# Roots refined on GpSimd, head scales applied to k, normalisation on ScalarE and a three-part output projection in a windowed-attention kernel

## The reference

```
_gn(v):    32 groups of 8 channels; (g - mean) / sqrt(var + 1e-5) per image and group
xw     = roll(x, -4, -4), cut into 8 x 8 windows: 4 windows per image, N = 64 tokens each
q, k   = xw @ Wq.T, xw @ Wk.T          (16 heads of 16 channels);   v = xw @ Wv.T + bv
qn, kn = q / max(|q|, 1e-12), k / max(|k|, 1e-12)
logits = (qn . kn) * exp(min(logit_scale, log 100)) + 16 * sigmoid(bias(head, n, m))
logits = -inf where the shifted-window mask says so;  scores = softmax(logits)
z      = (scores @ v) @ Wo.T + bo, rolled back
```

## Time and profile before

| | |
|---|---|
| median of 3 runs | 882.07 us (876.42 to 893.16) |
| the profiled execution: its own time | 888.09 us |
| its span, first to last instruction | 885.6 us |
| mean granted TensorE clock | 0.956 |
| busy share of the span: PE, PEld | 87%, 74% |
| busy share: DVE, ACT, POOL | 68%, 51%, 52% |

### The profile page before, as it was taken

The page is one execution under the profiler, slowest core; times in us unless marked ns, Lnnn a source line. Parts: engine busy times, 40 slices in busy tenths (PEclk is TensorE's granted clock), DMA queues, the critical chain, the costliest instruction groups (busy, mean ns, idle before and its releaser), DMA issues.

```text
span 885.6 us, 38114 instructions
## 1 busy us (share of the span) xinstructions
PE 767.5 (87%) x15258; PEld 654.2 (74%) x15258; DVE 606.6 (68%) x1641; ACT 453.1 (51%) x848; POOL 457.3 (52%) x584
## 2 busy tenths in 40 slices
PE   3086899999999999997999999999999999999985
PEld 2065778777877787776788887787778777788874
DVE  5164677777767777776777777777777777777641
ACT  2143555555555555653555555555655555555540
POOL 2015546555655665555466555565556555665540
PEclk9576999999999999998999999999999999999995
DMA  5706520000000000000000000000000000000000
GB/s 113 137 12 95 163 61 0 0 0 0 0 0 0 0 0 0 0 3 2 3 3 4 15 26 15 24 24 24 24 12 24 24 24 12 24 26 27 26 28 28
DMA packets 17197, 22.13 MB, mean 25 GB/s; under 512 B 7097, under 2 KB 8418, under 8 KB 17122
## 3 DMA queue, kind: packets, MB, share of 16 engines
q1 hardware_dynamic: 16578, 20.31, 8.8%
q10 hardware_dynamic: 544, 0.79, 0.3%
HBM read 12.68 MB, written 8.42 MB: 24 GB/s over the span
## 4 chain that ended last, share of the span: by engine, by line
PE 62%; DVE 15%; issue 9%; ACT 9%; SPq 3%; DMA 1%; ACTq 1%; DVEq 0%
PE ps_qk L365 21%; PE ps_mix L477 15%; PE ps_qk L489 12%; PE ps_score L450 9%; DVE ps_score L709 5%; ACT squares L553 4%; ACT seed L597 3%; PE ps_mix L467 2%; PE ps_score L410 2%; DVE ps_score L725 2%; DVE ps_score L727 2%; DVE ps_score L729 2%; ACT q_own L575 1%; DVE exp_bias L688 1%; DVE g_off L746 1%
## 5 line engine op out<-in xcount | busy, mean ns | idle before, releaser
L913 POOL TENSOR_TENSOR probs<-probs,exp_bias 128x512 f32<-128x512 f32 x256 | 326.4, 1306 | 267.5 <-ACT probs L612 257.5
L612 ACT ACTIVATE probs<-ps_score,lower 128x512 f32<-128x512 f32 x256 | 155.1, 689 | 128.2 <-PE ps_score L450 128.2
L365 PE MATMUL ps_qk<-w_qk,xn 128*128 128x512 f32 x768 | 205.0, 418 | 0.6 <-POOL xn L892 0.6
L365 PEld LDWEIGHTS ps_qk<-w_qk,xn 128*128 128x128 f32 x768 | 147.3, 199 | 32.3 <-POOL xn L892 0.7
L477 PE MATMUL ps_mix<-v_ones,probs 64*64 64x17 f32 x8064 | 134.3, 209 | 6.5 <-issue 6.5
L477 PEld LDWEIGHTS ps_mix<-v_ones,probs 64*64 64x64 f32 x8064 | 127.6, 136 | 8.7 <-issue 6.7
L553 ACT ACTIVATE squares<-ps_qk 128x512 f32<-128x512 f32 x128 | 76.6, 599 | 109.3 <-PE ps_qk L365 109.3
L398 PE MATMUL ps_mix<-mixed,w_o 128*128 128x256 f32 x512 | 131.0, 400 | 1.4 <-ACT mixed L567 1.4
L450 PE MATMUL ps_score<-q_own,k_rows 32*64 32x128 f32 x4096 | 78.4, 281 | 57.9 <-DVE g_off L746 56.8
L489 PE MATMUL ps_qk<-w_v,xn 128*128 128x256 f32 x768 | 109.4, 293 | 20.3 <-DVE unit L761 20.3
L450 PEld LDWEIGHTS ps_score<-q_own,k_rows 32*64 32x64 f32 x4096 | 63.4, 132 | 82.5 <-DVE g_off L746 50.1
(11 more groups left out here) (74 smaller groups left out, 766.7 us busy)
## 6 DMA issues: line engine op xcount, KB each, us to landing
x_all<-in_x SPq DMA_DIRECT2D x32, 256.0 KB, 2.9
out<-x_out SPq DMA_DIRECT2D x32, 256.0 KB, 2.0
bias_rev<-table_scratch SPq DMA_DIRECT2D x32, 56.5 KB
probs<-in_L_matrices ACTq DMA_DIRECT2D x1, 512.0 KB, 3.7
x_out<-in_L_matrices SPq DMA_DIRECT2D x1, 512.0 KB, 12.0
w_o<-in_L_matrices SPq DMA_DIRECT2D x4, 128.0 KB
probs<-in_L_matrices ACTq DMA_DIRECT2D x1, 256.0 KB, 4.2
allowed<-in_L_matrices SPq DMA_DIRECT2D x1, 256.0 KB, 11.7
```

Source lines behind the costliest of these rows:

```text
L365: last = nc.tensor.matmul(ps_qk[:, e, :], xn[:, px, t.parity, c, e * P:(e + 1) * P], w_qk[:, pw, t.layer, c, :], start=(c == 0 and i == 0) ...
L612: nc.scalar.activation(probs[:, t.parity, r, :, :, :, :].rearrange("p e c a n -> p (e c a n)"), ps_score[:, r, :], ACT.Exp, bias=lower[:, ...
L913: nc.gpsimd.tensor_tensor(pr, pr, exp_bias[:, t.layer, r, :, :, :, :].rearrange("p e c a n -> p (e c a n)"), ALU.mult).then_inc(weighted, 1)
```

## The change

Six edits come together.

1. `newton` moves to GpSimd, between `split_xn` and `weigh`. It has four tensor_tensor operations on up to 66 columns in place of three, on SBUF tiles (`sums_sq`, `seed`, `refined`, `root`, `threes`), each waiting for the one before, and one more for the group offset `g_off`. The squares are taken of twice the value, so that root = (3 - 4 s y^2) y needs no halves. `score` no longer waits for the roots.
2. The head scales are no longer folded into the roots (`scale_norms` is gone); `keep_k` multiplies the transposed k by them, one number per partition. `make_unit` does the clamp and the product in one operation.
3. `normalise` moves from VectorE to ScalarE, after the four `exp`.
4. `project_out` takes three rounded parts: 8 float32r products with the high part of `mixed`, then 4 with its low part, which a new VectorE operation `keep_rest` makes. The output weights are rounded on ScalarE and split on VectorE.
5. Orders: ScalarE does both `keep_q` ahead of `log_sums` and `seed_roots`; VectorE does both residuals ahead of `make_unit`. TensorE's `project_v` stands ahead of `mix` as it did.
6. Loops hold four iterations per pass (4 to 23 and 38 to 57). x2 and x3 are loaded ahead of the bias gathers, x4 too; the tables of both layers begin in the prelude, and `find_table(1)` of ScalarE, the rounding and the splits of layer 1 move to iteration 3.

The core of the diff:

```diff
@@ run
-                first = (4, IMAGES + 6)[layer]
-                last = IMAGES * (layer + 1) - 6
-                with engine.Fori((first + JOBS * exact) // 2, (last + JOBS * exact) // 2) as half:
-                    for parity in range(2):
-                        iteration(first + parity, Job(half, parity, None, exact))
-                some(last, last + (12, 10)[layer])
+                first, last, after = ((4, 24, IMAGES + 6), (IMAGES + 6, 58, JOBS + 4))[layer]
+                with engine.Fori((first + JOBS * exact) // 4, (last + JOBS * exact) // 4) as quarter:
+                    for k in range(4):
+                        half, parity = divmod(first % 4 + k, 2)
+                        iteration(first + k, Job(2 * quarter + half, parity, None, exact))
+                some(last, after)
@@ sync
-            load_table(0)
+            for l in range(LAYERS):
+                sp.dma_start(cpb1[:, l, :], weights[l]["cpb1"]).then_inc(table_in, 16)
+                sp.dma_start(cpb2[:, l, :], weights[l]["cpb2"]).then_inc(table_in, 16)
...
+            load_x(Job(1, 0, 0, 0))
+            load_x(Job(1, 1, 0, 0))
...
-                load_x(job(j, base, WARM + 2))
+                load_x(job(j, base, WARM + 4))
                 if j == -WARM and not base.exact:
-                    load_table(1)
                     spread_bias(0)
@@ tensor, project_out
+                pe.wait_ge(mixed_hi, t.count(1, 1))
+                for c in range(CC):
+                    for a in range(2):
+                        for part in range(2):
+                            nc.tensor.matmul(z_cols[:, c, :], w_o[:, part, t.layer, a, c * P:(c + 1) * P], mixed[:, 0, a, :],
+                                             start=(c + a + part == 0), stop=False, skip_group_check=True)
                 pe.wait_ge(mixed_ready, t.count(1, 1))
                 for c in range(CC):
                     for a in range(2):
-                        last = nc.tensor.matmul(z_cols[:, c, :], w_o[:, t.layer, a, c * P:(c + 1) * P], mixed[:, a, :],
-                                                start=(a == 0), stop=(a == 1), skip_group_check=True)
+                        last = nc.tensor.matmul(z_cols[:, c, :], w_o[:, 0, t.layer, a, c * P:(c + 1) * P], mixed[:, 1, a, :],
+                                                start=False, stop=(a == 1), skip_group_check=True)
@@ tensor, score
                 past(pe, exped, t.count(4, 0))
-                if job(j, base, 0) is not None:
-                    pe.wait_ge(rnorm_ready, job(j, base, 0).count(1, 1))
-                if job(j, base, 2) is not None:
-                    pe.wait_ge(gn_scaled, job(j, base, 2).count(2, 2))
@@ tensor, iteration
                 project_v(now)
                 mix(j, base, older)
-                if j == 0 and not base.exact:
-                    find_table(1)
@@ scalar
+            def round_out_weights(l):
+                act.wait_ge(out_in, 16 * OUT_IN)
+                nc.scalar.activation(w_o[:, 0, l, :, :], w_o_in[:, l, :, :], ACT.Copy).then_inc(w_hi, 1)
...
+            def normalise(u):
+                if u is None:
+                    return
+                act.wait_ge(gn_offset, u.count(1, 1))
+                past(act, xn_ready, u.count(1, 0))
+                for c in range(CC):
+                    nc.scalar.activation(xn32[:, c, :], x_all[:, bass.ds(u.image, 1), c, :].rearrange("p o t -> p (o t)"), ACT.Identity,
+                                         bias=g_off[:, c:c + 1], scale=root[:, 2 * NORMS + c:2 * NORMS + c + 1]).then_inc(xn32_ready, 1)
@@ scalar, iteration
                 keep_mixed(oldest)
+                keep_q(before, 0)
+                keep_q(before, 1)
                 log_sums(j, base)
-                keep_q(before, 0)
                 seed_roots(j, base)
-                keep_q(before, 1)
                 keep_shift(before)
                 for r in range(GROUPS):
                     exp(before, r)
+                normalise(job(j, base, 2))
                 keep_v(now)
@@ vector
+                by = scales[:, t.layer, :].rearrange("p (o c u) -> p o c u", o=1, u=1).broadcast_to([P, 2, CC, P])
+                nc.vector.tensor_tensor(k_rows[:, :, :, :], k_turned_to, by, ALU.mult).then_inc(k_ready, 1)
+
+            def keep_rest(t):
...
+                nc.vector.tensor_tensor(mixed[:, 1, :, :], back_cols, mixed[:, 0, :, :], ALU.subtract).then_inc(mixed_ready, 1)
+
+            def make_unit(base, t, e):
+                if t is None:
+                    return
+                dve.wait_ge(newton_step, chain(base, ROOT_OPS, ROOT_OPS))
                 past(dve, k_turned, t.count(1, 0))
...
+                by = root[:, e * NORMS:(e + 1) * NORMS].rearrange("p (h o) -> p h o", o=1).broadcast_to([P, NORMS, HD])
+                nc.vector.scalar_tensor_tensor(out=unit[:, e, :].rearrange("p (h d) -> p h d", d=HD), in0=by, scalar=INV_NORM_TOP,
+                                               in1=ps_qk[:, e, :].rearrange("p (h d) -> p h d", d=HD), op0=ALU.min, op1=ALU.mult).then_inc(unit_ready, 1)
@@ vector, iteration
-                sum_norms(now, 0)
-                sum_norms(now, 1)
+                sum_norms(base, now, 0)
+                sum_norms(base, now, 1)
+                keep_rest(oldest)
                 keep_k(before)
-                newton(j, base)
-                scale_norms(j, base, now)
-                scale_groups(j, base, after)
-                make_unit(now, 1)
-                make_unit(now, 0)
                 add_residual(oldest, 0)
                 add_residual(oldest, 1)
                 refine_shift(before)
                 cap(before)
-                normalise(after, 0)
-                normalise(after, 1)
+                make_unit(base, now, 1)
+                make_unit(base, now, 0)
                 divide(older)
@@ gpsimd
+            def newton(j, base):
+
+                t, u = job(j, base, 0), job(j, base, 2)
+                if t is None and u is None:
+                    return
+                at = root_columns(t, u)
+                step = lambda n: pool.wait_ge(newton_step, chain(base, ROOT_OPS, n))
+                pool.wait_ge(seeded, chain(base, 1, 1))
+                nc.gpsimd.tensor_tensor(refined[:, at], sums_sq[:, at], seed[:, at], ALU.mult).then_inc(newton_step, 1)
+                step(1)
+                nc.gpsimd.tensor_tensor(refined[:, at], refined[:, at], seed[:, at], ALU.mult).then_inc(newton_step, 1)
+                step(2)
+                nc.gpsimd.tensor_tensor(refined[:, at], threes[:, at], refined[:, at], ALU.subtract).then_inc(newton_step, 1)
+                step(3)
...
+                nc.gpsimd.tensor_tensor(root[:, at], refined[:, at], seed[:, at], ALU.mult).then_inc(newton_step, 1)
+                step(4)
+                if u is not None:
+                    nc.gpsimd.tensor_tensor(g_off[:, :], root[:, 2 * NORMS:], neg_mean[:, :], ALU.mult).then_inc(gn_offset, 1)
...
                 split_xn(job(j, base, 1))
+                newton(j, base)
```

More of the change, by code:

```diff
@@ L112, in build @@
         w_v = sb("w_v", [P, 2, L, CC, D], F32R)
-        w_o = sb("w_o", [P, L, 2, D])
+        w_o_in = sb("w_o_in", [P, L, 2, D])
+        w_o = sb("w_o", [P, 2, L, 2, D], F32R)
         v_bias = sb("v_bias", [P, L, 2])
@@ L312, in iteration @@
                 if j == -WARM and base.exact:
-                    load_x(job(j, base, WARM))
-                    load_x(job(j, base, WARM + 1))
-                load_x(job(j, base, WARM + 2))
+                    for k in range(4):
+                        load_x(job(j, base, WARM + k))
+                load_x(job(j, base, WARM + 4))
                 if j == -WARM and not base.exact:
-                    load_table(1)
                     spread_bias(0)
@@ L333, in _ @@
         def _(pe):
-            def find_table(l):
-                pe.wait_ge(table_in[l], 16 * TABLE_IN[l])
-                nc.tensor.matmul(ps_score[:, 0, 0:REL * REL], cpb1[:, l, :], coords[:, :], start=True, stop=True).then_inc(hidden_done, 1)
+            pe.wait_ge(table_in, 16 * TABLE_IN)
+            for l in range(LAYERS):
+                nc.tensor.matmul(ps_score[:, l, 0:REL * REL], cpb1[:, l, :], coords[:, :], start=True, stop=True).then_inc(hidden_done, 1)
+            for l in range(LAYERS):
                 pe.wait_ge(hidden_ready, l + 1)
-                nc.tensor.matmul(ps_mix[0:HEADS, 0, 0:REL * REL], cpb2[:, l, :], hidden[:, l, :], start=True, stop=True).then_inc(table_done, 1)
+                nc.tensor.matmul(ps_mix[0:HEADS, l, 0:REL * REL], cpb2[:, l, :], hidden[:, l, :], start=True, stop=True).then_inc(table_done, 1)
             def sum_out_bias():
@@ L344, in sum_out_bias @@
                         for a in range(2):
-                            last = nc.tensor.matmul(ps_mix[:, 1, l * CC + c:l * CC + c + 1], w_o[:, l, a, c * P:(c + 1) * P], v_bias[:, l, a:a + 1],
```

(27 more changed lines are left out.)

136 lines of the change are left out of this document (50 added, 86 removed).

## The result

The changed kernel takes 927.5 us in the median of 4 runs (925.94 to 930.06) against 886.98 us for the kernel before (876.42 to 893.16): ratio 1.0552, 95% interval 1.048 to 1.0624. It is 5.5% slower. The profiled execution took 930.06 us, its span is 928.2 us.

The account below looks back on a forecast made before the run. Bound by the loop q and k, square, sum, log, seed, root, unit, v, mix. Steady state +27, loops -6, start -13, drain -1 make +7 on 888.1, 895; the median is 6 below, so 889 us, range 864 to 912.

Parts of the forecast that it names:

- Rival A: TensorE's loop of four iterations isn't held and each pass fetches instructions again: +16, so 905 us; chance 0.28.
- The forecast's own case: Loop of four held, jobs 0.45 us longer: 889 us, own range 876 to 902; chance 0.40.
- A's price: Fetch between `mix` and `project_qk` on each of 8 loop returns: 1 to 5.41 us, nearest 2, so +16.
- The wait moves from score to `project_v`: Score starts a microsecond earlier; `project_v` waits 1.4 us for unit vectors where score waited 0.69; job +0.45 us.
- GpSimd's operation, 0.33 from a line between 0.20 and 1.28: Each 66-column root step on GpSimd takes 0.33 us, interpolated between 4 and 512 columns; gap between steps 0.09 us.
- Output products hidden: The 12 output products take 1.64 us in place of 1.99; the 0.35 saved turns into waiting ahead of `project_v`.
- The start, -13: With x2 and x3 loaded ahead, first unit vectors come near 30 us, 13.5 earlier; together -13 us (-19 to -8).
- Loops, -6: Branches halve, register work stays; half of about 12 us over 42 loop jobs is saved: -6 (0 to -9).
- The drain, -1: At the end, three jobs whose output products are not hidden: -1 us.
- Rival B: Clock falls as PE idles after score, up to 1.7 us a job; ten more jobs hit, +17: 906; chance 0.10.
- Rival C: Roots are fast enough, `project_v` starts at or before 8.05, start and loop gains remain: 862 us; chance 0.17.
- Rival D: The start gives nothing back, another load or the bias gathers being late next: 903 us; chance 0.05.

Follow-up runs that it names:

- The shortened loop: The changed kernel with its loops of four, score issuing 4 of its 32 products in the loops: 986.89 us in one run.

## Why the prediction was wrong

The forecast was 889, no change, with a range of 864 to 912, and the kernel took 927.5. The step that failed is the one under the whole sum: that TensorE's loop of four iterations is held. The sum's one term for the loops was a saving, -6. Rival A, that the loop isn't held, was given a chance of 0.28 because no row shows the limit, and a price of 2 us a return. The runs showed that it isn't held, and 5 us a return.

The forecast's own case, with the loop held, is the version with loops of two on TensorE alone, and that measured 887.5. That the numbers meet is in part luck: +7 was forecast on a median of 882, and -2.5 was measured against 890, with terms off in both directions.

Between the profiled executions of the two kernels (spans 928.2 and 885.6), told by the starts of `make_unit`, the changed kernel is 15 us ahead at the sixth job; it loses 26 in the rest of the first loop (19 jobs) and 30 in the second (20 jobs), 3 in the written-out stretches, and wins 1.5 in the drain.

- *A's price.* The term was 8 x 2 = 16. It measured 40 in the changed kernel and about 50 in the kernel before. A return lasts 3.3 to 4.4 us, and the q and k projection behind it runs 1.3 to 2.4 us longer with the clock down. In the first loop (3.3 to 3.8 us) a single packet passes in each stall, and takes 0.9 to 1.3 us; around each stall of the second (4.1 to 4.4 us) there are two. So in the first loop more than 2 us of a stall is not a packet under way; what it is, no run shows. Both parts had a forerunner among the rows, a stop of 5.41 us for instructions and a clock that fell; the first was only A's far bound, the second was not added to it at all. Bodies of about 1000 and 1540 instructions are held, and one of about 2000 is not (242 products a job, two instructions each, four jobs, and the waits). Lengths between the last two weren't tried. The Trainium skill's rule (Runtime: NRT & Kernel Launch, "Instruction fetch mechanics") gives TensorE room for 2048 instructions and says that a taken branch outside what is held stalls. The stall agrees with the runs; the length only roughly, for the body that isn't held comes out just under that figure.
- *The wait moves from score to `project_v`.* Right in place, and in size 1.30 us of wait against 1.4. The job grew by 0.29 and not 0.45. After the start of `project_qk`, the seed ended at 5.94 (placed at 5.93) and `make_unit` started at 7.60 (7.65); `project_v` followed 0.74 behind that, where 0.85 was allowed for the first unit vectors and the release. These two, 0.05 and 0.11, are the whole difference.
- *GpSimd's operation, 0.33 from a line between 0.20 and 1.28.* Right: 0.33. The gap of 0.09 is 0.08.
- *Output products hidden.* Right in the job.
- *The start, -13.* The size was nearly right, the way to it not. The first unit vectors came at 33.6, 9.7 earlier and not 13.5. The first `project_qk` came 5.3 us later than in the kernel before (24.32 against 19.06) where 2 were allowed: the longer root chains and the rounding of w_qk, queued behind the new `normalise` on ScalarE. Another 5 came back behind them, where the changed kernel hasn't the stop of the earlier trace rows: by the sixth job it is 15 ahead. With loops of two on TensorE alone it is 9 ahead there, for that version has a stop of its own, 4.25 us.
- *Loops, -6.* With loops of four on all engines but TensorE a job in the loop takes about 12.8 against 12.47 written out: 0.3, no less than in the kernel before. Loops of two everywhere take 12.9, so the longer loops do save 0.1 a job, but in the changed kernel a loop of two costs more than it did before (0.45 a job over the written-out one, against 0.3).
- *The drain, -1.* 1.5.
- *Rival B.* In the changed kernel the clock falls behind each stall. On its own it was small here. The shortened loop shows how far it can go: 4.6 us a job, where 1.7 was set, because `mix` and `project_qk` both run slow.
- *Rival C* was false for this kernel and true for the one with roots on VectorE. *Rival D* was false: the start gave back what it was to give.

## What to carry to other kernels

Before a loop body is doubled, count the instructions of its longest stream, the products with their weight loads and passes, and look at the instruction queue's packets while a loop runs: none means that the body is held. Here the stream written out in full (870.73 us) was faster than the loop just too long (927.5) and than the loop of two (887.49). Behind an engine's idle wait there can be a second one; before taking the first away, find the one behind it and its slack. That slack, here 0.55 us, is all there is to gain until the second chain is shortened too, and a later log and small dependent steps on an engine that is slower per step spent it and 0.29 more.

## What the runs showed that I had not expected

- Less work on an engine can go with more time: without 28 of 32 score products a job, TensorE's idle time ahead of `project_v` rose from 1.3 to between 2.0 and 2.4 us, the granted clock in most of the first loop fell to 0.70, and jobs there went from 12.5 to 17.1 us.
- A return to instructions that aren't held costs 3.3 to 4.4 us with the DMA engines all but idle, of which, in the first loop, the one 16 KB packet takes 0.9 to 1.3; packets in sequence cost nothing measurable once the loads of the start are over.
- While those loads run, a stream in sequence can stop as well: 3.88 to 7.05 us, once, in each version with TensorE's loops of two, and 5.41 in the kernel before.
- Loops on ScalarE, VectorE, GpSimd and SyncE may well be twice as long as TensorE's: that was 10 us faster than equal loops of two.
